# Post-norm linear attention and butterfly FFN: GpSimd applies mean and rstd, late slots project queries first, the last normalizer stands in slot 35, and reciprocals are loaded two pairs at a time

## The reference

```python
q, k, v = split(x @ W_qkv)                     # 16 heads of 64
q, k = relu(q @ W_f + b_f), relu(k @ W_f + b_f)
kv = einsum('bhnd,bhne->bhde', k, v)
out = einsum('bhnd,bhde->bhne', q, kv)
out = out / (einsum('bhnd,bhd->bhn', q, k.sum(2)) + 1e-6)
x = layernorm(x + out @ W_out + b_out)
h = butterfly(x @ W_exp + b_exp)               # 9 stages over 512 features
h = gelu(h + up_bias)
x = layernorm(x + butterfly(h) @ W_con + b_con + down_bias)
```

## Time and profile before

| what | value |
|---|---|
| median of 3 runs | 366.74 us (366.02 to 367.36) |
| the profiled execution, its own time | 367.46 us |
| its span, first to last instruction | 365.6 us |
| PE busy | 325.9 us, 89% |
| DVE busy | 246.4 us, 67% |
| ACT busy | 173.0 us, 47% |
| GpSimd busy | 81.4 us, 22% (most of it before 98 us) |
| mean granted clock of PE | 0.969 |

### The profile page before, as it was taken

One profiled execution on the slowest core, in us unless ns is written; L12 is line 12 of the kernel. 1 busy time (PEld: TensorE's weight loads), 2 busy tenths in 40 slices (PEclk: granted clock), 3 DMA queues, 4 the chain that ended last, 5 costly groups with the idle time before them and its releaser, 6 DMA issues.

```text
span 365.6 us, 5158 instructions
## 1 busy us (share of the span) xinstructions
PE 325.9 (89%) x1841; PEld 230.7 (63%) x1841; DVE 246.4 (67%) x489; ACT 173.0 (47%) x289; POOL 81.4 (22%) x77
## 2 busy tenths in 40 slices
PE   4898999479979999999999999999997996978981
PEld 3765667257657677777766677577675674554540
DVE  2534999999995355866641876468657758678553
ACT  2532335223464555566462746374653654353340
POOL 3072483898500001100100110011002011011121
PEclk9999999969989999999999999999999998989996
DMA  6950608443550730090063005600560380390011
GB/s 188 284 171 2 227 2 265 155 151 121 128 108 3 160 74 0 6 225 7 2 159 75 0 2 124 138 2 3 126 135 2 88 176 0 86 207 0 0 44 45
DMA packets 25090, 33.74 MB, mean 92 GB/s; under 512 B 3656, under 2 KB 13928, under 8 KB 25064
## 3 DMA queue, kind: packets, MB, share of 16 engines
q1 hardware_dynamic: 24904, 33.38, 35.7%
q10 hardware_dynamic: 160, 0.03, 0.0%
HBM read 31.04 MB, written 2.36 MB: 91 GB/s over the span
## 4 chain that ended last, share of the span: by engine, by line
PE 55%; DVE 27%; issue 7%; DMA 4%; POOL 3%; ACT 2%; SPq 1%; POOLq 0%; DVEq 0%; ACTq 0%
PE ring L489 19%; PE kx_ps L561 9%; PE attn_ps L489 8%; DVE late L920 6%; PE ring L649 5%; PE ring L581 3%; PE desk L498 3%; DVE qn L1001 3%; PE ring L541 3%; DVE bias_row_term L936 2%; DVE stats L1010 2%; POOL rstd L468 2%; DVE k_total L975 2%; DVE y_dn L924 2%; DMA recips<-recip_rows 2%
## 5 line engine op out<-in xcount | busy, mean ns | idle before, releaser
L771 ACT ACTIVATE q<-ring,bf_col 128x512 f32<-128x512 f32 x64 | 44.0, 687 | 52.4 <-PE ring L489 52.1
L561 PE MATMUL kx_ps<-k,xs 128*128 128x512 f32 x128 | 60.2, 592 | 0.8 <-ACT k L764 0.8
L764 ACT ACTIVATE k<-ring 128x512 f32<-128x512 f32 x64 | 38.3, 599 | 34.2 <-PE ring L541 34.0
L907 DVE TENSOR_TENSOR qn_l<-qn,qn_h 128x512 fp32r<-128x512 f32 x64 | 42.8, 679 | 16.3 <-ACT qn_h L757 15.6
L757 ACT ACTIVATE qn_h<-qn 128x512 fp32r<-128x512 f32 x64 | 39.7, 627 | 27.4 <-DVE qn L1001 27.4
L465 POOL TENSOR_TENSOR var_eps<-mean_var,ln_eps 128x4 f32<-128x4 f32 x16 | 7.1, 444 | 191.1 <-DVE mean_var L1014 191.1
L457 POOL TENSOR_TENSOR y<-hid,y_up 128x512 f32<-128x512 f32 x18 | 38.9, 2180 | 38.9 <-DMA hid<-in_L_ffn_up_weights_dram 38.8
L1001 DVE TENSOR_TENSOR qn<-q,recips 128x512 f32<-128x512 f32 x64 | 41.1, 683 | 4.1 <-DMA recips<-recip_rows 3.9
L561 PEld LDWEIGHTS kx_ps<-k,xs 128*128 128x128 f32 x128 | 24.1, 189 | 19.2 <-issue 16.5
L489 PE MATMUL ring<-xT_h,wq_h 128*128 128x512 f32 x64 | 35.9, 560 | 0.0
L489 PE MATMUL ring<-wk_h,xT_h 128*128 128x512 f32 x64 | 29.7, 464 | 3.1 <-ACT q L771 2.1
(11 more groups left out here) (125 smaller groups left out, 541.3 us busy)
## 6 DMA issues: line engine op xcount, KB each, us to landing
recips<-recip_rows SPq DMA_DIRECT2D x32, 512.0 KB, 7.8
hid<-in_L_ffn_up_weights_dram SPq DMA_DIRECT2D x9, 512.0 KB, 4.9
x<-_L_ffn_down_weights_dram SPq DMA_DIRECT2D x9, 512.0 KB, 4.0
xs<-in_L_attn_x_dram SPq DMA_DIRECT2D x4, 512.0 KB, 6.7
out_dram<-y SPq DMA_DIRECT2D x8, 256.0 KB, 7.5
q<-in_L_attn_W_qkv_dram SPq DMA_DIRECT2D x2, 512.0 KB, 8.3
q<-in_L_attn_W_qkv_dram SPq DMA_DIRECT2D x2, 256.0 KB, 3.0
q<-in_L_attn_W_out_dram SPq DMA_DIRECT2D x2, 256.0 KB, 8.7
```

The costliest lines, as they stand in the source:

```text
L561: t_.matmul(kx_ps[half], xs[b % XBUF][:, t, :], k[kt % KRING][:, half * CH:(half + 1) * CH], start=t == 0, stop=t == TILES - 1).then_inc(s ...
L764: a_.activation(k[kt % KRING][:, half * CH:(half + 1) * CH], bank(("k", kt, half))[:, :], ACT.Relu).then_inc(s_taken, 1)
L771: a_.activation(q[:, i % QRING, :], bank(("q", i))[:, :], ACT.Relu, bias=bf_col[:, :])\
L907: v.tensor_tensor(dst, src, high.bitcast(fp32), ALU.subtract).then_inc(done, 1)
```

## The change

Five edits:

1. GpSimd applies mean and rstd itself (`normalise` in the new code), right after it has made rstd, for all chunks of the first norm and for chunks 0 to 6 of the second. The four DVE instructions stay only for chunk 7 of the second norm. Two waits are new on DVE: ahead of writing `mean_var` of chunk n it waits until chunk n-1 has been normalised, and `residual` waits for the chunk's x1.
2. From slot 28 on (`NO_KEYS`) PE projects both query steps ahead of the attention steps, and ACT relus both ahead of rounding `qn`.
3. The normalizer of chunk 7 moves from the head of slot 36 to slot 35, behind that slot's queries; its eps on ACT stands behind the first `qn_hi`, and its reciprocal on DVE behind the second `qn_lo`.
4. Reciprocals come in four loads of two pairs (each of two DMAs, one for each head of a pair) instead of two loads of four pairs. The buffer has the same size; the wait of a load for its free place counts in steps of two.
5. The ring's table follows edits 2 and 3.

```diff
-    RC = 4
+    RC = 2
@@
-    NORM_SLOT = {PAIRS // 2 * n + RECIP_AT: n for n in range(ALLCH)}
+    NORM_SLOT = {PAIRS // 2 * n + RECIP_AT: n for n in range(ALLCH - 1)}
+
+    LATE_NORM_SLOT = {PAIRS // 2 * (ALLCH - 1) + RECIP_AT - 1: ALLCH - 1}
+    NO_KEYS = ALLT - FIRST
@@
         order += [("q", i) for i in q_steps(s)[1:]]
+        if s in LATE_NORM_SLOT:
+            order.append(("norm", LATE_NORM_SLOT[s]))
@@
-                for half in range(2):
-                    g = 2 * n + half
-                    if g >= 2:
-                        sp.wait_ge(s_qn, RC * (g - 1))
+                for i in range(PAIRS // RC):
+                    if n:
+                        sp.wait_ge(s_qn, PAIRS * (n - 1) + RC * (i + 1))
                     for h in range(2):
...
+                        sp.dma_start(recips[h * D:(h + 1) * D, i, :, :],
+                                     rows[h, :, i * RC:(i + 1) * RC, :].to_broadcast([D, RC, CH]))\
+                            .then_inc(s_rc[i], 16)
@@ GpSimd
+            def normalise(i, n, dst, done):
+                pool.wait_ge(s_rs[i], n + 1)
+                for t in range(QUADS):
+                    ins = g.tensor_scalar(dst[:, t, :], dst[:, t, :], mean_var[i][:, t, 0:1], rstd[i][:, t:t + 1],
+                                          ALU.subtract, ALU.mult)
+                ins.then_inc(done, 1)
...
                 if s in ATT_T_SLOT:
-                    rstd_of(0, ATT_T_SLOT[s])
+                    n = ATT_T_SLOT[s]
+                    rstd_of(0, n)
+                    normalise(0, n, x1[:, n % X1BUF, :, :], s_x1)
                 if s in YT_SLOT:
-                    rstd_of(1, YT_SLOT[s])
+                    n = YT_SLOT[s]
+                    rstd_of(1, n)
+                    if n < ALLCH - 1:
+                        normalise(1, n, y[:, n % 2, :, :], s_yo)
@@ PE
+                if s >= NO_KEYS:
+                    for i in q_steps(s):
+                        project_q(i)
+                if s in LATE_NORM_SLOT:
+                    norm(LATE_NORM_SLOT[s])
                 for a in adds(s)[:1]:
                     add_attn(a)
-                for i in q_steps(s)[:1]:
-                    project_q(i)
+                if s < NO_KEYS:
+                    for i in q_steps(s)[:1]:
+                        project_q(i)
@@ ACT
+                if s >= NO_KEYS:
+                    for i in q_steps(s):
+                        q_relu(i)
                 for a in spreads(s)[:1]:
                     qn_hi(a)
-                for i in q_steps(s)[:1]:
-                    q_relu(i)
+                if s in LATE_NORM_SLOT:
+                    norm_eps(LATE_NORM_SLOT[s])
+                if s < NO_KEYS:
+                    for i in q_steps(s)[:1]:
+                        q_relu(i)
@@ DVE
-            def layer_norm(i, n, src):
+            def layer_norm(i, n, src, done):
                 for t in range(QUADS):
                     v.bn_stats(stats[i][:, t, :], src[:, t, :]).then_inc(s_st[i], 1)
                 dve.wait_ge(s_st[i], QUADS * (n + 1))
+                if n:
+
+                    dve.wait_ge(done, n)
                 v.memset(scratch[:, :], 0.0)
@@
             def residual(n):
                 dve.wait_ge(s_dmade, desk_of["y", n] + 1)
+                dve.wait_ge(s_x1, n + 1)
@@
                 for a in spreads(s)[1:]:
                     qn_lo(a)
-                if s in ATT_T_SLOT:
-                    layer_norm_end(0, ATT_T_SLOT[s], x1[:, ATT_T_SLOT[s] % X1BUF, :, :], s_x1)
+                if s in LATE_NORM_SLOT:
+                    reciprocal(LATE_NORM_SLOT[s])
                 if s in MAPS_SLOT:
                     m_lo(*MAPS_SLOT[s])
-                if s in YT_SLOT:
-                    layer_norm_end(1, YT_SLOT[s], y[:, YT_SLOT[s] % 2, :, :], s_yo)
+                if YT_SLOT.get(s) == ALLCH - 1:
+                    layer_norm_end(1, ALLCH - 1, y[:, (ALLCH - 1) % 2, :, :], s_yo)
```

More of the change, by code:

```diff
@@ L217, in postln_linear_attention_butterfly_ffn_kernel @@
         recip = sb("recip", [128, QT])
-        recips = sb("recips", [128, 2, RC, CH])
+        recips = sb("recips", [128, PAIRS // RC, RC, CH])
         recip_rows = nc.dram_tensor("recip_rows", [ALLCH, 2 * PAIRS, CH], fp32, kind="Internal").ap()
@@ L306, in postln_linear_attention_butterfly_ffn_kernel @@
         s_rst = sem("recip_stored")
-        s_rc = [sem(f"recips_{i}_loaded") for i in range(2)]
+        s_rc = [sem(f"recips_of_pairs_{2 * i}_loaded") for i in range(PAIRS // 2)]
         s_qn = sem("qn_done")
@@ L404, in spread @@
                 rows = recip_rows[n, :, :].rearrange("(o p h) t -> h o p t", o=1, h=2)
-                for half in range(2):
-                    g = 2 * n + half
-                    if g >= 2:
-                        sp.wait_ge(s_qn, RC * (g - 1))
+                for i in range(PAIRS // RC):
+                    if n:
+                        sp.wait_ge(s_qn, PAIRS * (n - 1) + RC * (i + 1))
                     for h in range(2):
-                        sp.dma_start(recips[h * D:(h + 1) * D, half, :, :],
-                                     rows[h, :, half * RC:(half + 1) * RC, :].to_broadcast([D, RC, CH]))\
-                            .then_inc(s_rc[half], 16)
+                        sp.dma_start(recips[h * D:(h + 1) * D, i, :, :],
+                                     rows[h, :, i * RC:(i + 1) * RC, :].to_broadcast([D, RC, CH]))\
+                            .then_inc(s_rc[i], 16)
             def store_out(n):
@@ L713, in _ @@
                     add_kx(kt)
-                for i in q_steps(s)[1:]:
-                    project_q(i)
+                if s < NO_KEYS:
+                    for i in q_steps(s)[1:]:
+                        project_q(i)
                 if s in MAPS_SLOT:
@@ L996, in normalise_q @@
                 if a % RC == 0:
-                    dve.wait_ge(s_rc[a // RC % 2], 32 * (a // RC // 2 + 1))
+                    dve.wait_ge(s_rc[a % PAIRS // RC], 32 * (a // PAIRS + 1))
                 if a >= 2:
@@ L1000, in normalise_q @@
                     dve.wait_ge(s_qnl, a - 1)
-                v.tensor_tensor(qn[:, a % 2, :], q[:, a % QRING, :], recips[:, a // RC % 2, a % RC, :],
+                v.tensor_tensor(qn[:, a % 2, :], q[:, a % QRING, :], recips[:, a % PAIRS // RC, a % RC, :],
                                 ALU.mult).then_inc(s_qn, 1)
@@ L1028, in add_x @@
                 dve.wait_ge(s_dtaken, desk_of["attn", n] + 1)
-                layer_norm(0, n, x1[:, n % X1BUF, :, :])
+                layer_norm(0, n, x1[:, n % X1BUF, :, :], s_x1)
             def residual(n):
                 dve.wait_ge(s_dmade, desk_of["y", n] + 1)
+                dve.wait_ge(s_x1, n + 1)
                 if n >= 2:
@@ L1037, in residual @@
                 dve.wait_ge(s_dtaken, desk_of["y", n] + 1)
-                layer_norm(1, n, y[:, n % 2, :, :])
+                layer_norm(1, n, y[:, n % 2, :, :], s_yo)
             def xT_lo(b, c):
```

## The result

The changed kernel takes 374.23 us, the median of four runs (371.86 to 376.93), against 366.38 us of the kernel before on the same chips: the ratio is 1.0227, 95% interval 1.0140 to 1.0314. It is slower by 2.3%, where 9.5 us less were forecast, and outside the range. The profiled execution is the fastest of the four, 371.86 us; its span is 369.9 us.

A forecast was written before the change was run, and what follows sets the result against it. PE's idle time and slow clock between slots 30 and 43, caused by DVE, put 14.2 us at stake; less 3.4 idle and 1.3 port loss, 9.5 us won: 357.2 us by the median, range 354.5 to 360.5.

The forecast's parts named there:

- GpSimd normalises: Norms moved from DVE to GpSimd: 2.2 us off DVE per norm, 13.2 us between slots 30 and 43.
- where x1 is waited for: PE's x1 transposes: x1 ready 3.0 to 5.8 us after statistics; hidden for chunks 4 and 5, 1.3 us wait for chunk 6.
- The sum: From slot 30 on: 14.2 us at stake, less 3.4 idle and 1.3 for the port, gives 9.5 us won.
- The capacity is there: GpSimd has room for four added instructions per norm, 0.35 us each, 1.4 us together.
- the bracket: Duration of one new GpSimd instruction: 0.29 us from below, 1.27 us from above, 0.35 taken.
- Rival B: Slower: DVE waits for GpSimd's four instructions at 1.27 us each; +8 us, 375 us; chance 0.07.
- B's point of decision: The kernel gets slower once a GpSimd instruction takes about 0.9 us, where half the net loss exceeds the order's gain.
- the mutual exclusion that the prediction counted on: GpSimd instructions and DVE's two-SBUF-input ones alternate: up to 1.4 us lost to DVE per norm, GpSimd through after 4.2.
- A: Rival: the port takes back what DVE won, at about 0.57 us per instruction; only 4.4 us won, 362.3 us; chance 0.12.
- the early reciprocal: Chunk 6's reciprocal on DVE comes about 4 us earlier, two norms of 2.2, so the 3.93 us wait goes.
- the relu wait of slot 35: Chunk 7's normalizer, moved to slot 35, makes PE wait one relu, taken as 0.7 us.
- Queries first: From slot 28 on, query steps ahead of attention steps: the 2.4 us wait ahead of normalizer 6 goes.

The follow-up runs named there:

- e11: The changed kernel with GpSimd's four instructions for x1 left out, so x1 stays without mean and rstd: 354.83 us, ratio 0.9700 to the kernel before.
- e3: The changed kernel with the first norm (x1) applied on DVE and only the second (y) on GpSimd: 359.07 us, ratio 0.9773 to the kernel before.
- e4: The kernel before with only the queries moved first from slot 28 on: 369.21 us, ratio 1.0050.
- e5: The changed kernel with x1 on DVE, y on GpSimd, and attention and query steps alternating again in slots 28 to 34: 357.79 us, ratio 0.9756.
- e9: The changed kernel with each GpSimd normalise instruction cut into two of 64 columns: 385.87 us, ratio 1.0533 to the kernel before.

## Why the prediction was wrong

**The failed step is "GpSimd normalises", in the part "where x1 is waited for".** Three things in it were wrong, all for one result, x1:

- The cover. "For chunks 4 and 5 the transpose has 3 us or more of PE work ahead of it (slots 32 and 36, with a down product), and hides it." The cover was there, 3.6 and 6.2 us, although slot 32 has no down product; but 3 us do not hide a delay that the same paragraph puts at 3.0 to 5.8. At 5.8 us PE would have waited 2.2 us for chunk 4 and, with 2.7 us of cover, 3.1 for chunk 6. The sum had 0 and 1.3; PE waited 4.66 and 4.07.
- GpSimd's queue. In slots 30 and 31 a y norm stands directly ahead of an x1 norm. "The capacity is there" was true of the average, and x1 of chunk 4 was taken up 2.3 us late all the same. This term was missing; it is chunk 4's alone, since GpSimd was idle ahead of the norms of chunks 5 and 6.
- The duration. "A quarter of that is 0.32, and I take 0.35": 0.79 us undisturbed. I scaled the two-input instruction of the earlier trace rows by columns, as if it had no fixed part, and took the select of the earlier trace rows for the same kind of work. The measured value lies inside the bracket (0.29 and 1.27); the one taken was not argued, only convenient. In the tail this is the whole of the 1.7 us that was put at 0. In the stretch it weighs less: with 0.35 and full alternation a disturbed norm had 4.2 us, and the three took 4.50, 5.46 and 4.45.

Behind them stands the clock. The sum took the slow stretches as gone, and the new waits brought them back. The stretch is 13.0 us over its forecast: 8.2 more of idle PE (11.6 instead of 3.4) and 6.1 more of busy time (66.8 instead of the 60.7 at full speed), less the 1.3 that DVE was to lose to GpSimd, of which nothing is seen.

That GpSimd's work on x1 is nearly the whole of the error is shown from both sides: without it the stretch is 64.2 us (e11), and with x1 back on DVE and all else in place it is 67.3 (e3). How the delay divides into the instruction's own time, its meeting with DVE and the queue is read from the rows of one execution; no run separates them. One that lets GpSimd take x1 ahead of y wasn't made.

**Which case came true.** Rival B said slower, with its place (the four instructions) and a price of 8 us; 7.9 were measured. That the number fits is luck. B had DVE waiting for GpSimd, and DVE did not wait. These are its `qn` from 146 us on, where the new instructions are:

```profile
L1031 DVE TENSOR_TENSOR qn<-q,recips x50: 677/684/777, 149.3 to 333.6; 128x512 f32<-128x512 f32 x50
```

Before, the median was 683 ns and the longest 693. In the last third PE's new waits name GpSimd, not DVE; GpSimd was the one that waited where the two met. B's point of decision, 0.9 us for an instruction, leaves out the tail that B prices beside it; with the tail at 4 x (t - 0.35) B's own sum turns at 0.78 us, about the undisturbed 0.79, and then gives no loss to speak of. Beside the new instructions the mutual exclusion that the prediction counted on shows on GpSimd's side only: 4.50 us beside `qn_l` and `qn`, 3.12 us without. So the cost to DVE that A needs did not come either.

**What was right.** The bound (PE idle between slots 30 and 43, at DVE's hand), the early reciprocal (3.5 us for two norms, where 2.2 each were worked out), the relu wait of slot 35, no time lost ahead of slot 30, and a stretch of about 65 us once x1 is in time. Missed was chunk 0, for whose x1 PE waits 1.59 us; the prediction had no wait for the norms ahead of slot 30.

**What was right for another reason.** I counted the gain as the order's and DVE's together. Queries first alone made the kernel 0.5% slower (e4), and taken out of the fast version nothing is lost (e5). There the 2.4 us ahead of normalizer 6 are gone without the new order, so they were a symptom of DVE's delay, not a cost of its own.

## What to carry to other kernels

When work moves to a slower engine, ask for each result how long after its inputs it is there, not whether the engine has time, and set that delay against the work that the waiting engine has in between, chunk by chunk. Here the same four instructions won 1.2% where only a store waited for them and lost 1.1% in sum when x1 went along. Count in that latency what stands ahead in the new engine's queue at that very place, and an instruction's fixed part, which scaling by columns leaves out. And a wide bracket is no reason to take its lower end: where the forecast turns on a value between 0.3 and 1.3 us, the forecast at both ends belongs into the chances.

## What the runs showed of the hardware

A GpSimd instruction that subtracts and multiplies with two per-partition scalars took 0.57 us for 64 columns and 0.79 us for 128, which is 0.36 us and 3.4 ns per element on a straight line (e9). By this line the 128 elements alone take 0.43 us, more than twice the prediction's estimate for them. The instruction with two tensor inputs took 1.27 us for 512 columns, so 2.5 ns per element at most. DVE does the 128 columns in 0.34 us and overlaps four to 1.1 us.

Where these instructions met DVE's two-input ones, GpSimd lost and DVE didn't: GpSimd's went from 0.79 to up to 2.18 us, DVE's `qn` kept its median of 684 ns. In one place GpSimd had even begun first: at 331.77 DVE starts two `qn_l` 0.4 us behind GpSimd's first instruction and takes 1.29 us for them, as it does elsewhere (280.89). Beside GpSimd's instruction with two tensor inputs it was otherwise. `wup_l` began 0.4 us ahead of a `qn`, took 1.58 us instead of 1.27, and that `qn` is the only long one of the run:

```profile
143.02 1.58 POOL L488 TENSOR_TENSOR wup_l<-y_up,wup_h 128x512 fp32r<-128x512 f32 x1 [45.61 <-ACT wup_h L780]
...
143.38 1.77 DVE L1031 TENSOR_TENSOR qn<-q,recips 128x512 f32<-128x512 f32 x1
```

It alone makes most of the rise of `qn`'s mean from 683 to 706 ns. Why DVE waited here and not beside the new instructions is not shown.
